# A transformer tower for 16 images on one core: another order for the first five images, and for the last steps of the last image

## The reference

```python
gray = sum over channels of x * (0.2989, 0.587, 0.114)
h = (|conv3x3(gray, scharr_x)| + |conv3x3(gray, scharr_y)|) / 2      # [16, 256 tokens, 256]
n = layernorm(h)
Q = n @ W_dq @ W_uq;  K = n @ W_dkv @ W_uk;  V = n @ W_dkv @ W_uv    # 16 heads of 16, latent 64
h = h + softmax(causal(Q K^T / 4)) V @ W_o
out = h + layernorm(h) @ sign(W_ffn)^T
```

## Time and profile before

| | us |
|---|---|
| median of 3 runs (lowest to highest) | 435.75 (434.21 to 435.9) |
| the profiled execution | 436.89 |
| its span, first to last instruction | 435.1 |
| PE busy | 368.5 (85%) |
| DVE, ACT, POOL busy | 288.9, 238.9, 172.0 |
| moved by DMA | 74.13 MB, 170 GB/s over the span |

### The profile page before, as it was taken

How to read it: one execution, slowest core, us unless ns; L and a number is a source line. 1 busy time by engine, 2 the same in 40 slices (tenths; PEclk the granted TensorE clock), 3 DMA queues, 4 the chain that set the end, 5 groups by cost and what they waited for, 6 DMA issues and landing times.

```text
span 435.1 us, 9881 instructions
## 1 busy us (share of the span) xinstructions
PE 368.5 (85%) x3545; PEld 261.5 (60%) x3588; DVE 288.9 (66%) x539; ACT 238.9 (55%) x408; POOL 172.0 (40%) x367
## 2 busy tenths in 40 slices
PE   0335686999999999999999999999999989796764
PEld 0122364666676767676767676767676757574442
DVE  2224176886868687868686868686878776775520
ACT  2123425666767676767676767676757563534301
POOL 7032022545554546454545454545434323212200
PEclk9998669799999999999999999999999989898975
DMA  5966797959596878787878787675753534200000
GB/s 173 226 157 149 181 257 203 269 171 257 174 245 187 230 209 220 208 223 202 219 202 223 202 224 201 199 210 160 203 151 102 145 108 132 88 27 1 26 24 24
DMA packets 72266, 74.13 MB, mean 170 GB/s; under 512 B 6387, under 2 KB 66075, under 8 KB 72219
## 3 DMA queue, kind: packets, MB, share of 16 engines
q1 hardware_dynamic: 71355, 73.11, 61.5%
q10 hardware_dynamic: 864, 0.39, 0.3%
HBM read 51.98 MB, written 21.04 MB: 168 GB/s over the span
## 4 chain that ended last, share of the span: by engine, by line
PE 75%; DMA 7%; issue 5%; ACT 5%; DVE 4%; SPq 1%; POOL 1%; ACTq 0%; POOLq 0%
PE bank L910 14%; PE bank L1034 8%; PE bank L971 7%; PE bank L921 7%; PE bank L998 6%; PE bank L947 4%; PE bank L937 4%; PE bank L903 4%; PE bank L956 3%; PE bank L973 3%; PE bank L1037 3%; PE bank L1000 3%; PE bank L1015 3%; PE bank L984 3%; DMA q_st<-top_rows 3%
## 5 line engine op out<-in xcount | busy, mean ns | idle before, releaser
L628 ACT ACTIVATE probs<-bank 128x1024 f32<-128x1024 f32 x64 | 65.2, 1018 | 50.9 <-PE bank L1000 50.2
L774 DVE TENSOR_REDUCE top<-bank 128x4 f32<-128x1024 f32 x64 | 78.0, 1219 | 19.6 <-PE bank L973 19.5
L784 DVE TENSOR_TENSOR bank<-bank,cap_kq 128x512 f32<-128x512 f32 x64 | 44.7, 698 | 23.0 <-PE bank L1015 21.6
L971 PE MATMUL bank<-k_st,q_st 96*128 96x256 bf16 x256 | 48.3, 283 | 2.8 <-DMA k_st<-qk_parts 2.8
L921 PE MATMUL bank<-rows,band 102*32 102x256 f32 x512 | 34.1, 411 | 17.4 <-DMA rows<-gray_padded 17.4
L998 PE MATMUL bank<-q_st,k_st 99*128 99x256 bf16 x256 | 47.3, 278 | 1.0 <-DMA q_st<-top_rows 0.8
L1034 PE MATMUL bank<-probs,v_ring 128*32 128x256 f32 x512 | 42.4, 403 | 3.9 <-DVE rest L761 1.9
L779 DVE TENSOR_REDUCE top<-bank 128x4 f32<-128x512 f32 x64 | 41.6, 649 | 0.0
L471 POOL TENSOR_SCALAR var<-mv 128x2 f32<-128x2 f32 x16 | 3.6, 227 | 95.2 <-DVE mv L816 95.2
L633 ACT ACTIVATE probs<-bank 128x512 f32<-128x512 f32 x64 | 38.0, 594 | 3.8 <-DVE bank L784 3.6
L791 DVE STREAM_TRANSPOSE u<-bank 128x256 f32<-128x256 f32 x64 | 28.7, 448 | 11.1 <-PE bank L1037 5.9
(11 more groups left out here) (97 smaller groups left out, 750.9 us busy)
## 6 DMA issues: line engine op xcount, KB each, us to landing
x_sb<-in_x SPq DMA_DIRECT2D x16, 768.0 KB, 6.0
rows<-gray_padded SPq DMA_DIRECT2D x48, 256.0 KB
qk_parts<-parts SPq DMA_DIRECT2D x48, 256.0 KB, 3.1
q_st<-qk_parts SPq DMA_DIRECT2D x96, 128.0 KB, 3.0
k_st<-qk_parts SPq DMA_DIRECT2D x96, 128.0 KB, 3.0
gray_padded<-gray SPq DMA_DIRECT2D x16, 258.0 KB, 3.1
out_dram<-z SPq DMA_DIRECT2D x16, 256.0 KB, 3.0
rows<-gray_padded SPq DMA_DIRECT2D x32, 24.0 KB
```

The lines of the kernel that those rows point to most:

```text
L628: nc.scalar.activation(probs[:, g, :, 0:S], ps_k0, ACT.Exp, scale=SCALE).then_inc(exp0_done, 1)
L774: nc.vector.tensor_reduce(top[:, 1, g // 2, :, g % 2], ps_hi, AX.X, ALU.max, negate=True).then_inc(max_hi_done, 1)
L784: nc.vector.tensor_tensor(ps_k1, ps_k1, cap_kq[:, :].unsqueeze(1).to_broadcast([P, G, P]), ALU.min).then_inc(capped, 1)
L971: nc.tensor.matmul(ps_hi[:, i, :], q[:, hh, P:S], k[:, hh, :], start=(i == b * two), stop=False, skip_group_check=True)
```

## The change

The loops' middle stays in the same order. What differs:

- **SP:** the weights for Q, K, V (five transfers) and the rows of ones (three) are issued by ACT. Gray images 2 and 3 are stored ahead of the parts of image 0, and the first half of its operands is loaded before `load_rows(2)`. The first four of the six transfers of `load_operands` no longer wait for the third parts. The loads of x 4 and 5 and of W_ffn and W_o come after all the operands of image 1. In every later pass `load_x(i+5)` stands behind `load_operands(i+1)` instead of ahead of it.
- **Images 0 and 1:** DVE does the sum of the edges, the statistics and both small steps (`sum_and_scale`), POOL only the power; second and third parts go by halves.
- **Filters:** those of image 2 write banks 3 and 4 and move from pass -1 to pass 0.
- **Image 2** gets its transposes and projections in pass 1 (with image 3's), V of image 1 is made in pass 0. The signs of W_ffn are made in pass 2.
- **Constant products:** `keep_warm(36)` ahead of the first filters, 10 after filters 0, 10 in pass -1 after V of image 0, 5 ahead of the last W_o product and 8 after the feed forward of image 14. They write bank 5 from constants and nobody reads them.
- **Last images:** in passes 15 to 17 `measure_y` follows `add_y` at once. From image 13 on `turn_y` writes bank 0. In pass 17 `project(15)` stands ahead of `feed_forward(14)`, in banks 2 and 1; its y and z are done by token halves, and z is stored in two transfers.

```diff
             def load_operands(n, hf):
-                sp.wait_ge(third_out[n % 2], 16 * (n // 2 + 1))
                 need(sp, k1_done, NG * (n - ST_RING + 1))
                 for j in range(len(FROM_Q)):
+                    if j == 2:
+                        sp.wait_ge(third_out[n % 2], 16 * (n // 2 + 1))
...
+            store_gray(0)
+            load_rows(0)
+            store_gray(1)
+            load_x(2)
+            load_rows(1)
+            load_x(3)
+            store_gray(2)
+            store_gray(3)
+            store_parts(0)
+            store_third(0)
+            load_operands(0, 0)
+            load_rows(2)
+            load_operands(0, 1)
+            load_rows(3)
+            store_parts(1)
+            store_third(1)
+            load_operands(1, 0)
+            load_operands(1, 1)
+            load_x(4)
+            load_x(5)
+            load_outputs()
...
+            first_gray(0)
+            first_gray(1)
+            load_projections()
+            set_ones()
+            both_edges(0)
+            normalize_x(0)
+            first_gray(2)
+            copy_xt(0)
+            copy_c(0)
+            first_gray(3)
+            first_part(0)
+            second_part_halves(0)
+            both_edges(1)
+            copy_v(0)
+            normalize_x(1)
+            copy_xt(1)
+            copy_c(1)
+            first_part(1)
+            second_part_halves(1)
...
+            rest_of_gray(0)
+            rest_of_gray(1)
+            make_band()
+            make_up()
+            sum_and_scale(0)
+            rest_of_gray(2)
+            rest_of_gray(3)
+            rest_of_parts(0)
+            third_part_halves(0)
+            sum_and_scale(1)
+            rest_of_parts(1)
+            third_part_halves(1)
...
+            def sum_and_scale(n):
+                for t in range(T):
+                    dve.wait_ge(abs_done, T * n + t + 1)
+                    nc.vector.tensor_tensor(h_ring[:, n % H_RING, t, :], edge[:, t, 0, :], edge[:, t, 1, :],
+                                            ALU.add).then_inc(h_done if t else top_h_done, 1)
...
             def project(n):
                 pe.wait_ge(at_done, T * (n + 1))
+                if n == IMAGES - 1:
+                    pe.wait_ge(max_lo_done, NG * IMAGES)
+                    product(ps_y_last, a_t[:, n % 2, :, :], w_out, proj_done, top_proj_done)
+                    return
                 need(pe, z_done, upto(n - 1))
...
+                if i == LAST - 1:
+                    keep_warm(5)
+                    project(i - 2)
                 if live(i - 3):
                     feed_forward(i - 3)
+                if i == LAST - 1:
+                    keep_warm(8)
...
+            def keep_warm(count):
+                for _ in range(count):
+                    nc.tensor.matmul(bank[:, 5, :], ident_bf[:, :], mask_qk[:, :, :], start=True, stop=True)
```

More of the change, by code:

```diff
@@ L61 @@
 ON_VECTOR = 2
+BY_SCALAR = 5
 def live(n):
@@ new lines, in _ @@
+            load_operands(1, 0)
[3 more added lines that the diff above has]
+            load_outputs()
+            for i in range(1, LAST + 1):
+                if live(i + 1):
+                    store_parts(i + 1)
+                if i == 1:
+                    store_gray(4)
+                if live(i + 1):
+                    store_third(i + 1)
+                if i == 1:
+                    load_rows(4)
+                if live(i + 1):
+                    load_operands(i + 1, 0)
+                    load_operands(i + 1, 1)
+                if live(i + 5):
+                    load_x(i + 5)
+                if live(i + 4):
+                    store_gray(i + 4)
+                if live(i - 3):
+                    store_z(i - 3)
+                if live(i + 4):
+                    load_rows(i + 4)
@@ L657, in _ @@
                     exp_second(i - 1, 0)
-                if live(i + 1):
+                if i == 1:
+                    copy_xt(2)
+                    copy_c(2)
+                elif live(i + 1) and i:
                     second_part(i + 1)
@@ L671, in _ @@
                     exp_second(i - 1, 1)
-                if live(i + 4) and i > 0:
+                if i == 1:
+                    first_part(2)
+                    first_gray(4)
+                    second_part(2)
+                    copy_v(2)
+                    normalize_x(3)
+                if live(i + 4) and i > 1:
                     scale_colors(i + 4)
-                if live(i + 2):
+                if live(i + 2) and i > 1:
                     copy_xt(i + 2)
@@ L679, in _ @@
                     exp_second(i - 1, 2)
-                if live(i + 2):
+                if i == 1:
+                    copy_xt(3)
+                    scale_colors(5)
+                if live(i + 2) and i:
                     copy_c(i + 2)
-                if live(i):
+                if live(i) and i:
                     copy_max_rows(i, 0)
@@ L1100, in _ @@
                     lo_scores(i, 1)
-                if live(i + 2):
+                if i == 1:
+                    values(0, 0)
+                    expand_v(2)
+                if i == 0:
+                    expand_v(1)
+                    filters(2)
+                    turn_max(0, 0)
+                if live(i + 2) and i not in (0, 1):
                     turn_x(i + 2)
-                if i == 1:
-                    pe.wait_ge(signed, 1)
-                    pe.wait_ge(v_copied, 3)
-                    turn(ps_w, signs, turned)
+                if i == LAST - 1:
+                    keep_warm(5)
+                    project(i - 2)
                 if live(i - 3):
                     feed_forward(i - 3)
+                if i == LAST - 1:
+                    keep_warm(8)
                 if live(i - 1):
@@ L1116, in _ @@
                     lo_scores(i, 2)
+                if i == 1:
+                    turn_x(3)
                 if i == -2:
                     pe.wait_ge(weights_in, 3 * 16)
-                if live(i + 2):
+                if i == 2:
+                    pe.wait_ge(signed, 1)
+                    pe.wait_ge(v_copied, 4)
+                    turn(ps_w, signs, turned)
+                if live(i + 2) and i:
                     compress(i + 2)
```

274 lines of the change are left out of this document (158 added, 116 removed).

## The result

| | before | after |
|---|---|---|
| median of 20 runs (lowest to highest), us | 435.91 (434.21 to 440.28) | 432.93 (428.46 to 436.96) |
| ratio after/before, 95% interval | | 0.9895 (0.9863 to 0.9927) |
| profiled execution, span | 436.89, 435.1 | 428.94, 426.0 |

The kernel became faster by 1.05%, some 4.6 us; 416 us were forecast, in a range of 409 to 426. The side was right, the size was not: 432.93 lies 6.9 us outside the range. The medians are over all 20 runs, while the ratio leaves out the four of after that lie more than 1.5% above its fastest and stands for 4.6 us where these medians differ by 3.0.

The account below looks back on a forecast made before the run. Prediction: transfers bound the start, PE the middle, a chain of single steps the end. Gains of 8.5 (start) and 12.0 (end), 20.5 together, take the profiled 436.89 to 416.4, median 415.3; it said 416, range 409 to 426.

Parts of the forecast that it names:

- end: Last images: earlier statistics, W_o of image 15 first and halves end the span at 423.1 instead of 435.1, 12.0 us gained.
- start: Up to image 2's first scores: earlier operands and a shorter pass 1, less 2.0 for signs in pass 2; 8.5 us gained.
- middle: Later passes: load_x(i+5) goes behind twelve operand issues, about 7.6 us of SP; slack falls from 15 to 7 to 8; no effect.
- the landing of image 1's operands: Start: transfers set when image 1's scores begin, 61 us (60 to 62) instead of 70.31, 9.3 earlier.
- The first scores of image 0: Start: they would begin at 43 to 44 us instead of 55.92, 12 us earlier.
- the gaps: Start, ahead of image 1's scores: times with an empty transfer queue, about 3, 1, 1, 2, and 1 to 2 for the last landing.
- pass 1, "23.4": The pass before image 2's first scores would take 23.4 us instead of 24.57, so image 2 begins at 84.4 instead of 94.88.
- my two large savings: Pass 1: PE's 3.93 us stall at cap(0,0) goes, and some 2 us of PE time lost to the lower clock.
- Statistics at once: Last images: y's statistics right behind its sum remove PE's 2.76 us stall at turn_y(13) and the clock's fall; 3.0 us gained.
- Rival 4: Middle passes: x arrives too late for scale_colors, each waits on ACT; slower, 441 us; chance 0.05.
- Rival 1: Start given back: 2.1 MB of x4, x5 and weights ahead of image 2's parts; front gains 3, 421 us; chance 0.20.
- Rivals 2 and 3: 2: the clock falls at the end, 422 us, chance 0.14. 3: that and the front given back, 427, chance 0.06.

Follow-up runs that it names:

- end alone: The kernel before with only the changes of the last images; median 420.85 us, ratio 0.9685 to the kernel before.
- experiment 5: The changed kernel with load_x(i+5) behind the operands in passes 1 and 2 only, ahead of them from pass 3 on; 423.12 us, ratio 0.9655.
- experiment 6: The changed kernel with the store of gray issued ahead of the load of x, both behind the operands; 428.28 us, ratio 0.9819.
- experiment 12: Experiment 9 with the parts of image 1 stored ahead of load_rows(3) instead of behind it; 417.87 us, ratio 0.9565.
- experiment 9: Experiment 5 plus twelve constant products in pass 0, ahead of the second group of scores of image 0; 418.73 us, ratio 0.9615.
- experiments 10: Experiment 5 without the 56 constant products of the start; 422.91 us, ratio 0.9742.
- experiment 11: Experiment 9 with W_ffn and W_o loaded in pass 1 behind image 2's operands instead of ahead of the loop; 423.88 us, ratio 0.9740.
- experiments 1: The changed kernel with load_x(i+5) ahead of load_operands(i+1) again in SP's loop; 426.73 us, ratio 0.9789.

## Why the prediction was right and wrong

| term | forecast, us | measured |
|---|---|---|
| end | -12.0 | -14.0 (end alone) |
| start | -8.5 | -1.3, within the error of 0 |
| middle | 0 | +10.5 (experiment 5 to after) |
| sum | -20.5 | -4.6 |

**The step that failed: "The middle".** It says that the issue of x is late by 7.6 us, that x has a slack of 15, "now 7 to 8. Nothing." As arithmetic this holds as long as SP is on time, and experiment 6 shows it: there x is issued later still, and between 100 and 330 us ACT waited for it only once by more than 0.3 us (1.27, at 101.74). What I did not ask is what stands behind x in the queue and who waits for it. Behind it is gray, for which SP itself waits before `load_rows`; its landing goes from 3.1 to 6.4 us. Seven passes in the trace that are 0.8 to 1.6 us longer are 8.6 of the 10.5 us; the other 2 are within the intervals of the two ratios. The trace of before held the decider, SP's spare time of 4.5 us a pass, in its waits. I counted a moved DMA as 7.6 us of its queue's time and never asked whether the queue had become the bound; I read PE's clock and busy share in the middle and concluded that its passes cost what they cost.

**The start: the landing of image 1's operands, mis-sized.** The first scores of image 0 were right to 1 or 2 us (44.85). For image 1 I had 9.7 MB at 246 GB/s, 39.4 us, and 8 us of gaps: 61. After moved 190 GB/s over the 54.8 us from 12.40 to 67.20, at a DMA share of 0.76. Per unit of share that is 250 GB/s, close to the 246 that I had used. That is partly luck, for the 246 came from a stretch with a share of 0.87, 283 per unit of share, and so had idle time in it already. What failed is the gaps: the DMA engines were idle 0.24 of the time, 13 us and not 8. The largest hole is this one:

```profile
30.00:35.00 5.00, 2.62 (x41) 1.32 (x37) 2.68 (x5) 2.33 (x5) 0.00 (x0) 1.00 0.16 52
```

x(3) was issued at 23.24 instead of 21.71, after 6.6 us of waiting for the landing of gray 1, and landed at 31.52, where I had 28.5 to 29.5; so gray 3 was stored at 33.65, after 4.8 us of waiting for DVE. At the landing of parts 1, which I had at 2, SP stood still for 5.35 us, which experiment 12 fills; the DMA engines still had work for most of it (share 0.77 over 53.42:58.77). The landing in experiment 9 allows 64.6. The other 2.6 us, up to 67.20, go with the clock: it was granted at 0.69 over 44.85:67.20, with filters of 3.64 and 3.33 us. The 2.87 us of waiting at 49.00 for `max_hi` do not explain them by themselves, since experiment 5 has the same wait (2.62) and its scores at 64.73, with the filters of image 3 at 1.93. I had set wait and clock at nothing, the transfers being what PE waits for; in experiment 5 they are nearly nothing, in after they are not.

The rows of image 0 came late as well, at 20.16 instead of 17.36. Their issue is at 11.05 instead of 10.37; beside them stood 0.33 MB of weights, now issued by ACT, and x(2), issued at 13.86 instead of 15.90. No run separates the two, and in experiments 10, 11 and 12, with the same transfers up to there, the rows came at 18.65 to 18.90. By the Trainium skill (DMA: Bandwidth & Descriptors, section "Issuing engines are not separate DMA queues") transfers issued by several engines run on the same 16 DMA engines and interleave. The later rows agree with that, but they do not show that the weights are what delayed them. x(3) covered the delay.

**The start: pass 1, "23.4".** It took 26.1 us between first scores [windows above]. Of my two large savings the stall of 3.93 us is gone: no idle time of PE over 1.6 us is left in the pass. The 2 us for the clock did not come: 0.87, as before 0.86, with PE busy 23.09 of 26.14 us. I had assumed that filled time would keep the level up, and it did not here. Nor would it have been enough: in experiments 6, 10 and 11 the level did stay up over this pass (granted clock 1.00, 1.00 and 0.99), PE was busy 20.25 to 20.67 us, and the pass still took 25.39, 25.09 and 25.21 us. So the clock is worth some 1 us of the pass and not 2; the rest of the miss is idle time of PE, 3.05 us in after and 4.4 to 5.1 in those three, in short waits where the sum had 1.5 in all. By the first exponentials the pass takes 24.6 to 27.7 us in all versions with the new start, and 22.8 to 23.4 in those with the old one, which has one image less to project in it. So part of what the front gained at image 0 was paid back in moved work.

**The end: right in its mechanism, its terms mis-sized.** `turn_y`'s stall went, the clock stayed at 1.00, `feed_forward(15)` took 1.99 us. "Statistics at once" was worth 7.4 and not 3.0, since two images profit, and the products behind are faster.

**The rivals.** Rival 4, x too late for ACT, is there in the trace of after, and yet is not the cause. ACT waits 0.6 to 1.4 us for x in nearly every one of these passes, as here:

```profile
234.92 0.63 ACT L592 ACTIVATE gray<-x_sb 128x512 f32<-128x512 f32 x1 [1.19 <-DMA x_sb<-in_x]
```

This x was issued at 228.88, in a round that SP began late. But the chain between 160 and 240 us has no step of ACT among its longest and goes from landing to issue to landing, and the gray image made from that x is stored only in SP's next round, after 251.13. It is the slack of x eaten up by a late SP, an effect of the slow passes. A reader who looks at ACT's waits alone would confirm rival 4 from them. Rival 1 had the front given back to 3, which is close to what the front did (1 to 3), but not for its reason: in experiment 11 the weights ahead held image 2's operands by 0.4 us at most, and x4 and x5 were not tried. Rivals 2 and 3 did not occur, and no rival had x's neighbours in the queue. A piece of that chain of after, start, us, what:

```profile
206.71 6.18 DMA gray_padded<-gray
...
215.43 5.05 DMA qk_parts<-parts
220.50 0.55 SPq L344
```

## What to carry to other kernels

When a transfer is moved in a queue, look at the one that comes directly behind it and at who waits for that landing; the moved transfer's own slack answers another question. Before calling a queue free, add up one round of it and read its waits by kind: waits for work are its slack, waits for landings are not. And fill the wait for a landing with the issue of something big that is needed later, as x did before. `load_rows(3)` in experiment 12 does the same, but its rows are needed soon, and PE waited 1.96 us for them.

## What the runs showed of the hardware

A store of 258 KB takes 3.1 us from issue to landing (median) when only loads of 128 KB are issued ahead of it, and 6.4 us when a load of 768 KB is issued 0.6 us ahead of it, in another direction and with no data in common (x itself: 5.5 and 6.0); with the order reversed the store takes 3.8 and the load 7.3. A large neighbour ahead costs the store 3.3 us, more than its own landing.

Two executions of the same middle part can differ by a dip of the clock that nothing in the change accounts for: the pass from the first exponential of image 13 to that of image 14 takes 20.4 us in after and in experiments 1, 9 and 10, and 21.9 to 22.0 in before and in all the others, with the same work. The granted clock of that pass is 1.00 in after and 0.92 in experiment 5. In both PE stood idle for 1.90 us before it (at 360.77 and 350.35), waiting for the same step of DVE; then one kept its level and the other did not. The start scatters more: with the same order on all engines, five profiled kernels reached the first scores of image 1 between 64.73 and 69.37 us, the two quickest at a granted clock of 1.00 between 62 and 70 us, the two slowest at 0.57. What decides it stays open in both.
